# Toeplitz filter blocks of an attention layer stored as two bands of 32 output columns, each with its own range of rows

## What is computed

```
local_s = _fir(v_direct, fir_s)      # 3 taps
local_m = _fir(v_direct, fir_m)      # 15 taps
local_l = _fir(v_direct, fir_l)      # 63 taps
o = probs[..., 0:1] * local_s + probs[..., 1:2] * local_m + probs[..., 2:3] * local_l + probs[..., 3:4] * delta_out + probs[..., 4:5] * v_direct
```

## Time and profile before

| | us |
|---|---|
| median of 3 runs | 722.14 (715.11 to 724.0) |
| the profiled execution | 716.96 |
| its span in the trace | 715.0 |

### The profile page before, as it was taken

How to read it: one execution, slowest core, us unless ns; L and a number is a source line. 1 busy time by engine, 2 the same in 40 slices (tenths; PEclk the granted TensorE clock), 3 DMA queues, 4 the chain that set the end, 5 groups by cost and what they waited for, 6 DMA issues and landing times.

```text
span 715.0 us, 20289 instructions
## 1 busy us (share of the span) xinstructions
PE 567.2 (79%) x7980; PEld 454.8 (64%) x7980; DVE 482.9 (68%) x1166; ACT 283.0 (40%) x703; POOL 406.4 (57%) x503
## 2 busy tenths in 40 slices
PE   3788769768687676578989989989867678999964
PEld 2566546545574465467877878768766567788853
DVE  6999755434646353178798796797864666788863
ACT  2688831111535244043444443634513223444421
POOL 3211018546100298548998457899649999666522
PEclk9999979999979696699999998999989898999987
DMA  8749447995112610543213243031251111422201
GB/s 279 202 137 256 154 126 195 236 224 114 31 32 56 64 47 17 92 66 74 50 25 93 54 89 71 19 86 47 68 87 31 42 46 35 84 62 57 55 15 29
DMA packets 111149, 63.44 MB, mean 89 GB/s; under 512 B 81744, under 2 KB 104144, under 8 KB 109776
## 3 DMA queue, kind: packets, MB, share of 16 engines
q1 hardware_dynamic: 111056, 62.16, 37.6%
HBM read 43.18 MB, written 18.95 MB: 87 GB/s over the span
## 4 chain that ended last, share of the span: by engine, by line
DVE 26%; POOL 25%; PE 17%; issue 12%; DMA 11%; SPq 7%; ACT 2%; POOLq 0%; DVEq 0%; ACTq 0%
POOL seq L573 7%; DMA arena<-fms 6%; POOL seq L571 6%; POOL arena L582 5%; DVE arena L1160 5%; DVE cva L1042 4%; DVE arena L1257 3%; SPq L367 3%; PE bank L1729 3%; PE bank L1541 2%; PE bank L1611 2%; PE bank L1645 2%; POOL arena L544 2%; POOL arena L594 2%; DVE arena L1245 2%
## 5 line engine op out<-in xcount | busy, mean ns | idle before, releaser
L1160 DVE SCALAR_TENSOR_TENSOR arena<-bank,small,arena 128x256 f32<-128x256 f32 x192 | 91.4, 482 | 25.7 <-ACT arena L816 20.8
L582 POOL TENSOR_TENSOR arena<-arena,neg_half 128x2 f32<-128x2 f32 (+1 forms) x64 | 61.5, 961 | 74.2 <-DVE arena L1252 54.3
L573 POOL TENSOR_TENSOR seq<-seq 128x31 f32<-128x31 f32 (+15 forms) x124 | 86.7, 699 | 9.7
L571 POOL TENSOR_TENSOR seq<-seq 128x31 f32<-128x31 f32 (+15 forms) x124 | 69.4, 560 | 7.9
L1541 PE MATMUL bank<-arena 128*64 128x192 f32 x512 | 51.4, 345 | 16.9 <-DMA arena<-fms 13.3
L1134 DVE TENSOR_TENSOR seq<-bank,seq 128x384 f32<-128x384 f32 x64 | 35.2, 557 | 43.4 <-PE bank L1541 33.2
L502 POOL TENSOR_TENSOR seq<-seq 128x256 f32<-128x256 f32 x32 | 23.2, 726 | 68.0 <-DVE seq L1134 63.0
L816 ACT ACTIVATE arena<-bank,small 128x256 f32<-128x256 f32 x64 | 30.4, 475 | 58.6 <-PE bank L1611 58.5
L528 POOL TENSOR_TENSOR arena<-seq,powers 128x16 f32<-128x16 f32 x16 | 47.3, 2956 | 10.7 <-DVE seq L1169 10.7
L1541 PEld LDWEIGHTS bank<-arena 128*64 128x64 f32 x512 | 35.5, 142 | 27.5 <-DMA arena<-fms 15.7
L1611 PE MATMUL bank<-arena,w_q 128*128 128x268 f32 x128 | 37.5, 429 | 15.0 <-DVE arena L1160 14.9
(11 more groups left out here) (159 smaller groups left out, 1422.3 us busy)
## 6 DMA issues: line engine op xcount, KB each, us to landing
arena<-fms SPq DMA_DIRECT2D x16, 640.0 KB, 13.4
arena<-fl SPq DMA_DIRECT2D x16, 512.0 KB, 10.9
arena<-xnT_scratch SPq DMA_DIRECT2D x32, 134.0 KB, 2.8
gram_scratch<-arena SPq DMA_DIRECT2D x16, 256.0 KB, 2.3
arena<-v_scratch SPq DMA_DIRECT2D x32, 128.0 KB, 3.1
arena<-x SPq DMA_DIRECT2D x64, 64.0 KB, 2.2
out<-arena SPq DMA_DIRECT2D x64, 64.0 KB, 2.1
xnT_scratch<-seq SPq DMA_DIRECT2D x2, 1027.0 KB, 8.5
```

The source lines that it names most:

```text
L571: pool.tensor_tensor(part, below, above, ALU.mult).then_inc(s["solve"], 1)
L573: last = pool.tensor_tensor(into, into, part, ALU.add)
L582: pool.tensor_tensor(dst, src, half8 if k == U else neg_half[:, 0:k], ALU.pow).then_inc(s[dst_sem], 1)
L1160: nc.vector.scalar_tensor_tensor(cv[:, t], ps[:, :, j:j + C], conv_w[:, 1 - t // 2, t % 2, j:j + 1], cv[:, t], ALU.mult, ALU.add).then_inc ...
```

## The change

The 64 output columns of a Toeplitz block are cut into two bands of 32 columns. In band h only the rows from 32h on that a filter can reach are kept: 94 rows (2 to 95, counted from 32h) for the long filters and 46 rows (50 to 95) for the other two. The slot in `toep` gets a band dimension, `load(g)` issues four DMAs instead of two, all of `toep` is zeroed once in stage A instead of rows 0 to 47 of two filters, and a matmul reads its 192 columns as 2 x 3 runs of 32 instead of 3 runs of 64, and writes them to the same places as before. The numbers of matmuls, products and sums stay as they are.

```
-MS0 = 48
+BAND = C // 2
 ROWS = 2 * P - C
+LONG, SHORT = (2, 96), (50, 96)
...
-        toep = arena[:, A_V:A_V + A_T].rearrange("p (i f c t) -> p i f c t", i=NB, f=NF, c=GC)
+        toep = arena[:, A_V:A_V + A_T].rearrange("p (i s f c t) -> p i s f c t", i=NB, s=2, f=NF, c=GC)
...
             def load(g):
-                sp.dma_start(toep[:, g % NB, 0], fl[g]).then_inc(s[f"toep{g % NB}_in"], 16)
-                sp.dma_start(toep[MS0:P, g % NB, 1:3], fms[g]).then_inc(s[f"toep{g % NB}_in"], 16)
+                for h in range(2):
+                    sp.dma_start(toep[BAND * h + LONG[0]:BAND * h + LONG[1], g % NB, h, 0], fl[g, h]).then_inc(s[f"toep{g % NB}_in"], 16)
+                    sp.dma_start(toep[BAND * h + SHORT[0]:BAND * h + SHORT[1], g % NB, h, 1:3], fms[g, h]).then_inc(
+                        s[f"toep{g % NB}_in"], 16)
...
-                    pool.memset(toep[0:MS0, 2 * b:2 * b + 2, 1:NF], 0.0).then_inc(s["toep_zero"], 1)
+                    pool.memset(toep[:, 2 * b:2 * b + 2], 0.0).then_inc(s["toep_zero"], 1)
...
-                    pe.wait_ge(s[f"toep{g % NB}_in"], 32 * (g // NB + 1))
+                    pe.wait_ge(s[f"toep{g % NB}_in"], 64 * (g // NB + 1))
...
-                out_ = bank[fir_bank(q)][:, 0:2 * ROW].rearrange("p (f w) -> p f w", f=NF)
+                out_ = bank[fir_bank(q)][:, 0:2 * ROW].rearrange("p (f k s t) -> p k s f t", f=NF, k=2, s=2)
...
-                        last = mm(out_[HH[i], :, 64 * hh:64 * hh + C], vwin[:, P * pr + 64 * hh + d, :],
-                                  toep[:, g % NB, :, cin, :], start=True, stop=True)
+                        last = mm(out_[HH[i], hh], vwin[:, P * pr + 64 * hh + d, :],
+                                  toep[:, g % NB, :, :, cin, :], start=True, stop=True)
...
-        return rows.reshape(ROWS, FG, GC)[at].transpose(2, 0, 3, 1)
+        whole = rows.reshape(ROWS, FG, GC)[at].transpose(2, 0, 3, 1)
+        return np.stack([whole[:, BAND * h + rows_of[0]:BAND * h + rows_of[1], :, BAND * h:BAND * h + BAND] for h in range(2)], axis=1)
```

More of the change, by code:

```diff
@@ L1899, with padded @@
     order = np.arange(D).reshape(PAIRS, 2, 2 * C // GC, GC // 2).transpose(0, 2, 1, 3).reshape(D)
-    def padded(f):
+    def padded(f, rows_of):
         taps = f.reshape(D, -1)[order].T
@@ L1924 @@
             *(per_head(g[k]) for k in ("attn_gate_b", "attn_log_temp", "attn_eps_param"))], axis=1),
-        "fl": padded(g["attn_fir_l"]),
-        "fms": np.stack([padded(g["attn_fir_m"]), padded(g["attn_fir_s"])], axis=2)[:, MS0:],
+        "fl": padded(g["attn_fir_l"], LONG),
+        "fms": np.stack([padded(g["attn_fir_m"], SHORT), padded(g["attn_fir_s"], SHORT)], axis=3),
     }
```

## The result

The changed kernel takes 864.58 us (median of 4 runs, 856.38 to 868.08) against 721.16 us before (715.11 to 724.0): a ratio of 1.199, with a 95% interval of 1.187 to 1.210. It is slower by 143 us. The profiled execution took 856.38 us, its span is 854.5 us.

A forecast was written before the change was run, and what follows sets the result against it. The prediction took the filter stage to be bound by its loads from about 118 us on. It added 116 + 9 + 12 = +137 us to the profiled 717, giving 854, or 855 us for the median, range 818 to 905.

The forecast's parts named there:

- The rate of the loads: Filter loads of 94 and 46 rows run on 2 of 16 DMA engines, together 50 GB/s.
- The rival in which all 16 engines take part: Filter loads spread over all engines, PE sets the pace, about 707 us, faster by 2%; chance 6%.
- Both kinds of load on the same two engines: Long and short filters' loads share one pair of engines, 15.2 us a group; on separate pairs 7.7 us, chance 3%.
- The price of an engine: One DMA engine moves 25 GB/s in the filter loads, between 21.6 and 28.2, so a group takes 15.2 us.
- The rival with 15.6 GB/s: Two engines at their full-load rate, 24.4 us a group, about 1,000 us in all; chance 4%.
- Step 1: Filter loads of groups 4 to 15 take 186 us from first issue to last landing instead of 70.0: +116 us.
- Steps 2 and 3: Stage A: groups 0 and 1 delay sequence 3's rows, +9 us; groups 2 and 3 delay sequence 1's value stores, +12 us.
- Step 4: Twice as many load issues on SP, 2 x 0.4 us a group, hidden under the 15.2 us transfer: nothing.
- the prediction's sign of 30 us and more: In the filter stage the landing time of both kinds of filter load rises to 30 us and more.
- Step 5: Zeroing in stage A, 6144 instead of 4096 elements a partition, takes 1.8 us more each time: nothing.
- Step 6: Filter matmuls with runs of 32 columns cost nothing; even 5 us over 32 pairs would lie beneath the loads.
- The bytes: A filter group shrinks from 1152 to 744 KB; at 250 GB/s PE would set the pace, a gain of 15.5 us.

The follow-up runs named there:

- rows_96_48: The changed kernel with 96 and 48 rows in a band's loads instead of 94 and 46: 709.1 us, ratio 0.991 to the kernel before.
- rows_96_46: The changed kernel with 96 rows in the long filters' loads, the short ones' kept at 46: 766.4 us.
- rows_96_47: The changed kernel with 96 rows in the long filters' loads and 47 in the short ones': 880.02 us.
- split_80_14: The changed kernel with each load cut in two DMAs, of 80 + 14 and of 32 + 14 rows: 708.3 us, ratio 0.990 to the kernel before.
- late_only: The changed kernel with loads of 96 and 48 rows for groups 0 to 3, 94 and 46 rows for groups 4 to 15: 849.45 us.
- early_only: The changed kernel with loads of 94 and 46 rows for groups 0 to 3, 96 and 48 rows for the rest: 726.63 us.
- rows_96_48_zero_early: rows_96_48 with the zeroing moved, first half to POOL's start, second behind sequence 2's first power: 700.56 us, ratio 0.978 to the kernel before.
- before_zero_early: The kernel before with its own zeroing moved to POOL's start and behind sequence 2's first power: 715.26 us, ratio 0.995.

## Why the prediction was right, point by point

- **The rate of the loads: right, and shown.** Two engines, by the packets, the share of 0.14 to 0.15, the kernels with 46, 47 and 48 rows, and the loads cut at 80 + 14. The rival in which all 16 engines take part falls. The Trainium skill's rule (DMA: Bandwidth & Descriptors, section "Why a DMA increments its semaphore by 16 and not by 1") fits every count here: in the seven kernels with new loads (the changed one, rows_96_48, rows_96_46, rows_96_47, split_80_14, late_only, early_only) SP's queue has exactly the packets that it gives.
- **Both kinds of load on the same two engines: right**, though no row had shown it. A group takes 15.2 us, not 7.7.
- **The price of an engine: right.** 25 GB/s was the middle of two bounds, 15.2 us a group; measured 15.16, so 761,856 B / 15.16 us / 2 = 25.1 GB/s each. The rows gave only the bounds, 21.6 and 28.2 GB/s; that the middle hits within half a per cent is luck. The rival with 15.6 GB/s falls.
- **Step 1, groups 4 to 15: +116 forecast, +124.3 from the first filter matmul to the first projection.** From the first issue to the last landing it was 192.3 us (124.53 to 316.85), not 186. "With four slots the queue is never empty" was wrong: SP waits for the beta round trip, and the DMA share from 158 to 159 us is 0.00. PE's groups there start at 157.10 and 177.57 us, 20.5 apart instead of 15.2, which is 5.3 us. The windows' loads took 2.9 us instead of 1.3. Behind the last landing "as before" was 1.6 us short: 7.5 us to the first projection instead of 5.9, mostly because PE takes the first pair at the lower clock, 2.83 us instead of 1.52.
- **Steps 2 and 3, stage A: +21 forecast, +22.8 measured, but not from what I named alone.** early_only, with the same zeroing as rows_96_48, is 18.7 us later at the first filter matmul (118.47 against 99.78). The other 4.1 are the zeroing, 3.4, and the later landing of x. The two waits were where I had put them. The first is worth 6.8 us, not 9: the statistics of sequence 3 start at 63.40 us, against 56.62 in rows_96_48. That leaves 11.9 for the second, forecast 12.
- **Step 4, issues at nothing: the cost right, the reason wrong.** An issue took 3.7 us, not 0.4. It costs nothing only because it keeps step with the two engines. In stage A the same holding back kept the stores at SP. It also bounds the landing time: the prediction's sign of 30 us and more did not come, the loads in the chain land 18 to 19 us after their issue.
- **Step 5, zeroing at nothing: wrong.** I asked only whether SP and POOL had time. DVE was the engine beside it, on the path: 2.4 us of waiting there and 1.0 us on PE behind it.
- **Step 6, the new form of the matmul: right**, 1.52 us a pair as before in rows_96_48.
- **The bytes.** Worked out as 15.5 us if all engines take part. From the first filter matmul to the first projection rows_96_48 takes 70.3 us, against 81.6 before, 11.3 less; the later start takes 4.1 of that back, so its first projection comes 7.2 us earlier. rows_96_48_zero_early takes 66.4 us, 15.2 less than before, or 13.5 less than before_zero_early with 80.0. These are single executions, and what makes rows_96_48's stage 3.9 us longer than that of rows_96_48_zero_early was not tried.
- **The total.** The forecast for the profiled execution was 854 us, and it took 856.4. That this is so close is luck: up to the first projection the loss was 147 us instead of 137, and the last stretch was 7.6 us shorter for no reason that the change gives. The median, 864.6, is 9.6 over the 855 forecast.

## What to carry to other kernels

Before a transfer is trimmed, factor its leading counts: on SP's queue here a load of 94 rows ran on 2 engines, one of 96 on 16, and 47 rows on one. Round up to a multiple of 16 even if the added rows are zeros, or cut the load so that each piece divides well, and check it by the leftover packets or the DMA share in a stretch where only that load is in flight. And read what each neighbour engine does beside a long POOL instruction before it is called hidden, in its new place too.

## What the runs showed of the hardware that I had not expected

- Every DVE TENSOR_SCALAR in fp32 from on-chip memory to on-chip memory whose turn came during one of POOL's long MEMSETs was held until the MEMSET ended. It took 5.24 us instead of 0.41 beside one of 5.31 us, and 3.53 beside one of 3.60. BATCH_NORM_STATS2 was not held. Moving the MEMSET gave 3.3 and 5.4 us back. The Trainium skill describes this (SBUF — State Buffer, section "Who interferes with whom"): DVE in a two-port mode and GpSimd share one pair of ports, whoever starts first holds it for the whole instruction. The traces agree with the full block; that the mode is the reason no run here shows.
- SP is held at an issue while enough earlier loads are unfinished. The load issued at 204.74 us landed 18.28 us later in the chain of the changed kernel, while each took 3.8 us to transfer on its two engines (a quarter of a group's 15.16), so some five of them were in the queue:

```profile
204.74 18.28 DMA arena<-fms
```

- One slow pair of engines holds up DMAs that use all 16: the four value stores, 1 MB together, took 10.26 and 14.65 us to issue behind such loads instead of 3.65 and 4.18. By the packets each of them has a share of its bytes on those two engines.
